# Attention of one batch and second experts of the batch before it, interleaved in 64 steps in which TensorE takes the attention's share first

## What is computed

```python
x = x + selective_state_space_block(layernorm(x))
x = x + experts(layernorm(x))      # first experts
x = x + attention_b(layernorm(x))  # a linear ("flow") attention of 16 heads over 1024 tokens
x = x + experts(layernorm(x))      # second experts

# experts: every one of 16 experts is computed for every token
probs = softmax(x @ router_w.T + router_b); top_p, top_i = top_k(probs, 6)
for e in range(16):
    out = out + x @ expert_w[e] * gate[:, e:e + 1]
```

## Time and profile before

| what | value |
|---|---|
| median of 3 runs | 4711.26 us (4708.32 to 4712.44) |
| the profiled execution's time | 4707.32 us |
| its span, first to last instruction | 4705.3 us |
| mean granted TensorE clock | 0.97 |
| PE busy | 4300.6 us, 91% |
| DVE busy | 3605.8 us, 77% |
| ACT busy | 3070.8 us, 65% |
| POOL busy | 2587.7 us, 55% |

### The profile page before, as it was taken

The page is one execution under the profiler, slowest core; times in us unless marked ns, Lnnn a source line. Parts: engine busy times, 40 slices in busy tenths (PEclk is TensorE's granted clock), DMA queues, the critical chain, the costliest instruction groups (busy, mean ns, idle before and its releaser), DMA issues.

```text
span 4705.3 us, 83840 instructions
## 1 busy us (share of the span) xinstructions
PE 4300.6 (91%) x22592; PEld 2989.4 (64%) x22592; DVE 3605.8 (77%) x9602; ACT 3070.8 (65%) x8898; POOL 2587.7 (55%) x1284
## 2 busy tenths in 40 slices
PE   4899999999999999999999999876777799999999
PEld 4777777777777777777777777433443444444444
DVE  3899999999999999999999998633423367777776
ACT  5888888888888888888888888244444411111111
POOL 3988888888888888888888888300000000000000
PEclk8999999999999999999999999888888899999999
DMA  2111111111111111111111111100110000000000
GB/s 95 57 58 54 55 52 59 52 58 56 52 55 52 59 58 53 55 52 59 52 58 56 52 55 53 41 27 27 47 33 27 28 27 19 19 18 18 18 18 17
DMA packets 119138, 211.87 MB, mean 45 GB/s; under 512 B 19232, under 2 KB 85664, under 8 KB 118560
## 3 DMA queue, kind: packets, MB, share of 16 engines
q1 hardware_dynamic: 119072, 211.10, 13.7%
HBM read 184.83 MB, written 26.21 MB: 45 GB/s over the span
## 4 chain that ended last, share of the span: by engine, by line
PE 52%; issue 17%; DVE 17%; ACT 9%; POOL 2%; DMA 1%; DVEq 1%; SPq 1%; POOLq 0%; ACTq 0%
PE ps L654 26%; ACT zr L403 5%; PE ps L705 5%; PE ps L631 5%; DVE macc L964 3%; PE ps L781 3%; PE ps L684 2%; PE ps L691 2%; PE ps L760 2%; POOL prod L342 1%; PE ps_dA L781 1%; DVE xcv L1072 1%; DVE zt L1084 1%; PE ps L661 1%; DVE dtt L1121 1%
## 5 line engine op out<-in xcount | busy, mean ns | idle before, releaser
L654 PE MATMUL ps<-w_x,mxT 128*128 128x512 f32 x4096 | 1875.0, 596 | 8.9 <-DVE macc L964 8.9
L874 DVE TENSOR_TENSOR_SCAN hb<-ps_dA,hb 128x1088 f32<-128x1088 f32 x512 | 1240.7, 2423 | 76.3 <-POOL hb L350 65.3
L342 POOL TENSOR_TENSOR prod<-hb,cbc 128x1024 f32<-128x1024 f32 x512 | 1122.9, 2193 | 253.6 <-DVE hb L893 252.5
L350 POOL TENSOR_TENSOR hb<-u,bbc 128x1024 f32<-128x1024 f32 x512 | 1201.1, 2346 | 75.1 <-POOL prod L342 70.9
L403 ACT ACTIVATE zr<-dt,aneg 128x128 f32<-128x128 f32 x4096 | 1240.8, 388 | 1.4 <-DVE dt L1010 1.1
L964 DVE SCALAR_TENSOR_TENSOR macc<-ps,gate,macc 128x256 f32<-128x256 f32 x2048 | 977.4, 477 | 276.3 <-PE ps L654 203.7
L654 PEld LDWEIGHTS ps<-w_x,mxT 128*128 128x128 f32 x4096 | 736.3, 191 | 699.1 <-issue 632.1
L631 PEld LDWEIGHTS ps<-prod,ident 128*128 128x128 f32 x8192 | 948.8, 193 | 121.0 <-POOL prod L342 74.2
L631 PE MATMUL ps<-prod,ident 128*128 128x128 f32 x8192 | 966.7, 276 | 12.6 <-POOL prod L342 12.5
L412 ACT ACTIVATE ps_dA<-zr 128x1024 f32<-128x1024 f32 x512 | 518.4, 1012 | 0.0
L455 ACT ACTIVATE macc<-x1b,ms 128x256 f32<-128x256 f32 x128 | 64.1, 501 | 438.7 <-DVE macc L964 423.4
(11 more groups left out here) (186 smaller groups left out, 4876.7 us busy)
## 6 DMA issues: line engine op xcount, KB each, us to landing
bbc<-bcd SPq DMA_DIRECT2D x128, 512.0 KB, 3.7
cbc<-bcd SPq DMA_DIRECT2D x128, 512.0 KB, 3.7
xt<-in_x SPq DMA_DIRECT2D x128, 128.0 KB, 3.6
x2d<-macc SPq DMA_DIRECT2D x64, 128.0 KB, 1.7
xcv<-x2d SPq DMA_DIRECT2D x64, 128.0 KB, 2.1
x3d<-x1b SPq DMA_DIRECT2D x64, 128.0 KB, 1.9
x1b<-x3d SPq DMA_DIRECT2D x64, 128.0 KB, 2.0
out_dram<-macc SPq DMA_DIRECT2D x64, 128.0 KB, 1.7
```

The lines of the kernel that those rows point to most:

```text
L342: TT(dst, states, cc, ALU.mult).then_inc(M["prodp"], 1)
L350: TT(hb[c % 2][:].rearrange("p (e n) s -> p e n s", e=EB)[:, :, :, 1:SL], u[k][:, :, t0:t0 + CH].rearrange("p e (n s) -> p e n s", n=1).br ...
L654: last = mm(banks[p % len(banks)][:], mxT[k][:, j, :], w_x[:, j, p * 512:(p + 1) * 512], start=(j == 0), stop=(j == KD - 1))
L874: V.tensor_tensor_scan(states, dA, states, 0.0, ALU.mult, ALU.add).then_inc(M["scan"], 1)
```

## The change

Stages 2 and 3 become one. It has 9 rounds b = 0 to 8 of 64 steps ("slots") each, written out and not looped. In round b, slot s = 8 t + p holds the s-th share of the attention of batch b and pair p of the experts of tile t of batch b-1. Round 0 has no experts, round 8 no attention. Within a slot PE does the attention's share first, then the expert pair; DVE does the expert sums first, then the routing's share, then the attention's; ACT does the routing's share, then the attention's. The expert banks in rounds 1 to 7 are two (G0, G1), the attention has one set of four (`QUAD`) and M1 for small results. The input tiles of a whole batch (`x_rows`) and the attention's result (`x3_rows`) stay in SBUF, in buffers of stage 1: `x3d`, its 64 stores and 64 loads, and the second loading of `x2d` for the residual are gone. `co` is done before `ci`; `so` waits for `l1` since it uses the same banks. ACT loads its tables where the two functions alternate.

```diff
+        def merged(slot):
+            for b in range(NB + 1):
+                for t in range(NT):
+                    for p in range(X // 2):
+                        slot(b, t, p)
+
+        def routed(b, t):
+            n = (b - 1) * NT + t + 1
+            return n if 0 <= n < NTILES else None
...
+            def slot(b, t, p):                       # PE
+                n = (b - 1) * NT + t
+                if b < NB:
+                    attend(b, t * (X // 2) + p)
+                if b > 0:
+                    experts_mm(n + NTILES, n % 2, p, p + 1, G4 if b == NB else G, fresh=(b == NB and t == 0))
+                m = routed(b, t)
+                if m is not None:
+                    if p == 2:
+                        route(m + NTILES, m % 2, M0)
+                    if p == 3:
+                        logits(m + NTILES, m % 2, M0)
...
+            def attend(b, s):                        # PE
...
+                if s == 11:
+                    pe.wait_ge(A["hm"], AHEAD + (b + 1) * 4)
+                    columns_of(0, "cv0")
...
+                if s == 23:
+                    pe.wait_ge(A["hn"], AHEAD + (b + 1) * 4)
+                    pe.wait_ge(A["cv"], AHEAD + b + 1)
+                    columns_of(4, "cw0")
+                if s in (24, 25):
+                    by_group((0, 1) if s == 24 else (2, 3), (mats[:, 6, :], mats[:, 7, :]), ka, "co",
+                             lambda m: pe.wait_ge(A["l2"], AHEAD + b * 4 + m + 1))
+                if s in (29, 30):
+                    by_group((0, 1) if s == 29 else (2, 3), (mats[:, 4, :], mats[:, 5, :]), qa, "ci",
+                             lambda m: pe.wait_ge(A["cs"], AHEAD + b * 4 + m + 1))
+                if 35 <= s < 35 + NT:
+                    t = s - 35
+                    pe.wait_ge(A["v"], AHEAD + (b + 1) * KD)
...
+                if s in (47, 48):
+                    pe.wait_ge(A["kvm"], AHEAD + (b + 1) * KD)
+                    by_group((0, 1) if s == 47 else (2, 3), (mats[:, 8, :], mats[:, 9, :]), r1, "om", lambda m: None)
+                if 51 <= s < 51 + NT:
+                    t = s - 51
+                    pe.wait_ge(A["og"], AHEAD + (b + 1) * 4)
                     pe.wait_ge(A["x2"], AHEAD + b * NT + t - 1)
                     for j in range(KD):
                         last = mm((BC, YP)[t % 2][:, 0:D], r2[:, j, t * P:(t + 1) * P], w_a[:, 3, j, :],
                                   start=(j == 0), stop=(j == KD - 1))
                     last.then_inc(A["om2"], 1)
+                    if b + 1 < NB:
+                        transposes((b + 1) * NT + t)   # waits for A["xn"] of that tile
...
+            def slot(b, t, p):                       # DVE
+                n, r = (b - 1) * NT + t, routed(b, t)
+                if b > 0:
+                    expert_sums(n + NTILES, n % 2, 2 * p, 2 * p + 2, G4 if b == NB else G)
+                if r is not None:
+                    if p == 0:
+                        v.wait_ge(A["x3"], AHEAD + r + 1)
+                        route_norm1(r + NTILES, x3_rows(r))
+                    if p == 4:
+                        route_scores(r + NTILES, r % 2, M0)
+                    if p >= 5:
+                        for q in range(4 * (p - 5), min(4 * (p - 4), 11)):
+                            route_step(r + NTILES, q)
+                    if p == 7:
+                        route_gate(r + NTILES, r % 2)
+                if b < NB:
+                    attend(b, t * (X // 2) + p)
...
+            def attend(b, s):                        # DVE
...
+                if s in (17, 18):
+                    weighted(b, (0, 1) if s == 17 else (2, 3), qa, r1, "r1", "qs", 20)
+                if s in (20, 21):
+                    weighted(b, (0, 1) if s == 20 else (2, 3), ka, r2, "r2", "ks", 24)
+                if s == 22:
...
+                    head_masks(b, 4, (34, 35, 32, 33), "hn")
...
+                if s in (25, 26):                    # two of four clips, waits for "co", makes "cs"
...
+                if s == 27:                          # TS(xTa, xTa, -1.0, None, ALU.max)
...
+                if s in (28, 29):                    # half of the maximum each
...
+                if s == 32:                          # reciprocal of the sums "e"
...
+                if s in (33, 34):                    # half of v each, makes "v"
...
+                if s == 46:
+                    v.wait_ge(A["kv0"], AHEAD + b + 1)
+                    for j in range(KD):
+                        TT(mats[:, 8 + j, :], M1[:, j * P:(j + 1) * P], hmask, ALU.mult).then_inc(A["kvm"], 1)
+                if s in (48, 49):                    # two of four TT(r2, QUAD[m], r2), makes "og"
...
+                if b + 1 < NB and 50 <= s < 50 + NT:
+                    norm((b + 1) * NT + s - 50)
+                if b + 1 < NB and 48 <= s < 48 + NT:
+                    sums((b + 1) * NT + s - 48)
+                    moments((b + 1) * NT + s - 48)
+                if 52 <= s < 52 + NT:
+                    t = s - 52
+                    n = b * NT + t
                     v.wait_ge(A["om2"], AHEAD + n + 1)
+                    TT(x3_rows(n), (BC, YP)[t % 2][:, 0:D], bo_row[:], ALU.add).then_inc(A["x2"], 1)
                     v.wait_ge(A["x2"], AHEAD + n + 1)
+                    TT(x3_rows(n), x3_rows(n), x_rows(n), ALU.add).then_inc(A["x3"], 1)
```

More of the change, by code:

```diff
@@ L297, in _, with batch @@
             sp.dma_start(hmask, dram["hmask"]).then_inc(s_wc, 16)
[L299 to L325, removed]
+            def batch(b):
+                for n in range(b * NT, (b + 1) * NT):
+                    sp.dma_start(x_rows(n), flat_tile(x2d, n)).then_inc(A["x"][b % 2], 16)
+            batch(0)
+            for b in range(NB + 1):
+                if b + 1 < NB:
+                    sp.wait_ge(A["x3"], AHEAD + b * NT)
+                    batch(b + 1)
+                for n in range(max(b - 1, 0) * NT, b * NT):
+                    sp.wait_ge(R["ac"], AHEAD + (n + NTILES + 1) * (X + 1))
+                    sp.dma_start(flat_tile(out, n), macc[n % 2][:]).then_inc(R["o"][n % 2], 16)
             for k in range(2):
-                sp.wait_ge(A["o"][k], AHEAD + NTILES // 2 * 16)
-            experts(x3d, out, NTILES)
+                sp.wait_ge(R["o"][k], AHEAD + NTILES * 16)
         @block.gpsimd
@@ L612, in _, with ln_exp, sigmoid @@
-            for t in range(NT + 1):
-                norm(0, t)
-            with a.Fori(0, NB - 1) as b:
-                attend(b, True)
-            attend(NB - 1, False)
-            experts(NTILES)
+            table = ["ln"]
+            def ln_exp():
+                if table[0] != "ln":
+                    nc.scalar.preload_act_table_set("natural_log_exp_and_others")
+                table[0] = "ln"
+            def sigmoid(o, x, **kw):
+                table[0] = "sigmoid"
+                return act(o, x, ACT.Sigmoid, **kw)
@@ L620, in _ @@
+            for n in range(NT):
+                norm_scale(n)
+                if n > 0:
+                    norm_copy(n - 1)
+            norm_copy(NT - 1)
+            merged(slot)
         @block.tensor
@@ L736, in _, with by_group, columns_of, transposes @@
             pipeline(pe, step)
[L738 to L750 removed]
             pe.wait_ge(s_wa, 16)
[L753 to L757 removed]
+            def by_group(ms_, lhs, src, done, before):
+                for m in ms_:
                     j, g = m // NG, m % NG
                     before(m)
[L760 to L764 removed]
+                    mm(QUAD[m][:], lhs[j], src[:, j, g * TG:(g + 1) * TG], start=True, stop=True).then_inc(A[done], 1)
+            def columns_of(first, done):
+                for m in range(4):
+                    last = mm(M1[:, m:m + 1], mats[:, first + m, :], c_eps6[:], start=True, stop=True)
+                last.then_inc(A[done], 1)
+            def transposes(n):
+                t = n % NT
                 pe.wait_ge(A["xn"], AHEAD + n + 1)
@@ L829, in attend @@
                     last.then_inc(A["om2"], 1)
-                    if more and t > 1:
-                        transposes(b + 1, t - 2)
-                if more:
-                    transposes(b + 1, NT - 2)
-                    transposes(b + 1, NT - 1)
-            for t in range(NT):
-                transposes(0, t)
-            with pe.Fori(0, NB - 1) as b:
-                attend(b, True)
-            attend(NB - 1, False)
-            experts(NTILES)
+                    if b + 1 < NB:
+                        transposes((b + 1) * NT + t)
[9 more added lines that the diff above has]
+                        route(m + NTILES, m % 2, M0)
+                    if p == 3:
+                        logits(m + NTILES, m % 2, M0)
+            for n in range(NT):
+                transposes(n)
+            merged(slot)
         @block.vector
@@ L1265, in _ @@
+            for n in range(NT):
+                sums(n)
+                moments(n)
+                if n > 0:
+                    norm(n - 1)
+            norm(NT - 1)
```

(5 more changed lines are left out.)

473 lines of the change are left out of this document (199 added, 274 removed).

## The result

The changed kernel takes 4804.07 us (median of 4 runs, 4803.46 to 4805.44), the one before 4711.05 us on the same chip (4 runs, 4708.32 to 4712.44): ratio 1.0199, 95% interval 1.0181 to 1.0216. It is 2.0% slower. Predicted were 4840 us (4720 to 4940), 2.7% slower. The profiled execution took 4805.44 us, its span is 4803.4 us, the mean granted clock 0.966.

The account below looks back on a forecast made before the run. PE, standing for DVE's slot before, was taken to bound merged rounds. Start 3052, round 0 87, six rounds 1362, seventh 216, last experts 115.4, switch 1, end 2.2: span 4835.6, so 4840 us (4720 to 4940).

Parts of the forecast that it names:

- the gain of 34 us per round: Merged rounds: most the change can bring if PE never waits, 172 us against 206.0 before.
- The work, 172 us: PE's work in a merged round at full clock: attention 56.8 us plus experts 115.4.
- Idle, 38 us: PE's waits per merged round for DVE's slot before, at `hn`, `v`, `kvm`, `og`, `xn` and six `x2`: sum 37.8.
- Clock, 17 us: Merged round: clock falls after PE's waits in slots 23, 35, 47, 51 and 53 to 58 cost 17 us, ends 0 and 30.
- Six rounds of 227: Six merged rounds, each work 172, idle 38 and clock 17 us, together 1362 us.
- Round 0, 87 us: Attention alone: 87 us instead of 90.6, as `co` before `ci` saves 3.4 and no residual loads are awaited.
- Seventh round and switch, 217: Last round with attention, without a next norm, 216 us, and 1 us for the switch to the last experts.
- Last experts and end, 117.6: After the merged rounds: experts of the last batch 115.4 us and the end 2.2.
- Table loads, banks, `x3d`: Two more ACT table loads a round are covered, two expert banks add nothing, `x3d` transfers were already hidden.
- Clock hardly falls: Rival: merged rounds idle as forecast, but the clock costs only 0 to 5 us each; 4725 to 4760 us, chance 0.20.
- Faster: Rival: DVE's slots don't hold PE, idle and clock together below 36 us a round; chance 0.10.
- Worse: Rival: clock at half through most of slots 23 to 30 and 47 to 58, 30 us a round or more; 4930 up, chance 0.12.

Follow-up runs that it names:

- experiment 1: Changed kernel, but in each slot PE does the expert pair first and the attention's share after it: 4551.48 us, ratio 0.9668 to the kernel before.
- experiment 7: Changed kernel with PE's pair first and `om2`, transposes and the next batch's statistics and norm one slot later: 4527.73 us, ratio 0.9621 to the kernel before.
- experiment 4: Changed kernel with 17 unused matmuls a round on PE ahead of the waits for `x2`: 4752.18 us, ratio 1.0094 to the kernel before.
- experiment 2: Changed kernel, but DVE does the attention's share before the sums and the routing: 4622.15 us, ratio 0.9818 to the kernel before.
- experiment 5: Changed kernel, but DVE does the routing last (sums, attention, routing): 4788.11 us, ratio 1.0174 to the kernel before.
- experiment 8: The kernel of experiment 7 with the routing last on DVE: 4531.59 us, ratio 0.9623 to the kernel before.
- experiment 9: The kernel of experiment 8 with the routing last on ACT too: 4546.07 us, ratio 0.9661 to the kernel before.
- experiment 10: The kernel of experiment 7 with the routing last on ACT alone: 4563.21 us, ratio 0.9694 to the kernel before.
- experiment 3: Changed kernel with `om2`, transposes and the next batch's statistics and norm one slot later, `x2` unmoved: 4657.56 us, ratio 0.9894 to the kernel before.

## Why the prediction was right

**Direction and mechanism: shown.** It said that waits one slot back eat the gain of 34 us per round, at `hn`, `v`, `kvm`, `og` and six times at `x2`, and that all are DVE's. The rows of after have these and little else, and the first experiment, which lengthens that distance by one pair, takes three quarters of the waiting away. Of the signs that the prediction named, one failed: the clock of the merged stage is 0.93, not below 0.9. That the time is off by only 36 us is in part luck: the seven merged rounds were put 46 us too long and the other terms 14 us too short.

**Point by point**, from the span 4835.6 forecast to 4803.4 measured, 32.2 less:

- *The work, 172 us.* Right: 174.5 with the clock at 0.99 (experiment 7), so a part of the 2.5 us can still be the clock's.
- *Idle, 38 us.* Measured 32.5 in round 4075.26 to 4293.70 (218.44 less 185.97). Forecast against measured: `hn` 5.9, 5.05; `v` 4.2, 2.96; `kvm` 2.8, 2.33; `og` with `xn` of slot 50 4.4, 2.31 + 0.18; `xn` of slot 51 0.9, 0.84; the six `x2` 3.5, 3.3, 3.7, 3.8, 3.1, 2.2 against 3.16, 2.90, 3.32, 3.46, 2.83, 1.91. Each `x2` is 0.3 to 0.4 short of its forecast: the sum was made of durations, but DVE's instructions start up to 0.1 us before the one ahead ends (the norm of 0.41 was followed after 0.33). Over the longer chain ahead of `v` it comes to more: from the end of slot 25's pair (4123.6) to `v` DVE took 23.2 us where the forecast had 24.7, and PE 20.3 where it had 20.4. Not forecast were 0.94 us for ACT's `mxT` and 0.27 for `mxn`: I had gone through the waits of `attend` alone, not those of the routing's `route` and `logits`. At `hn` it is another thing. From the end of slot 18's pair (4097.36) DVE took 13.8 us, more than the forecast's 12.8 to 13.2, with 1.52 of it idle until slot 20's pair was done; but PE took 8.7 and not 7.4, since a wait of 0.94 for `mxT` and the routing's products lie in these slots:

```profile
4100.24 0.62 PE L653 MATMUL ps_dA<-w_r,mxT 128*128 128x16 f32 x4 [0.94 <-ACT mxT L421]
...
4102.71 1.07 DVE L977 SCALAR_TENSOR_TENSOR macc<-ps,gate,macc 128x256 f32<-128x256 f32 x2 [1.52 <-PE ps L665]
...
4111.15 1.87 PE L761 MATMUL ps_dA<-c_eps,prod 128*128 128x1 f32 x8 [5.05 <-DVE prod L1179]
```

- *Clock, 17 us.* Round 220.0 less 174.5 of work less 32.7 idle (mean of six) leaves 12.8. (Half of five chances of 2.8 is 7.0 and not the 7.5 of the sum, which changes little.) A typical round has 11.5; one of the six took 225.4 with PE busy 192.7 in it. The loss lies between the ends 0 and 30, and the clock falls at most of the places where I expected it, as the 4110 and 4205 stretches show; behind `kvm` it stayed at 1.00 (4175 to 4185).
- *Six rounds of 227.* 1322.2 instead of 1362 (3149.57 to 4471.79). This is the term that made the prediction too high, by 40 us: 5.3 us of idle and 4.2 of clock too many a round, 2.5 of work too few.
- *The start.* The first projection is at 3054.06 (3052).
- *Round 0, 87 us.* 95.5. The 3.4 us for `co` before `ci` came: PE's wait for `v` fell from 10.0 to 6.6. But I had left out the one-slot distance of `x2` here, where no pair lies between: six waits of 1.4 took the place of seven for `mxn` of 0.7, 3.5 us more, and PE's busy time is 70.7 instead of 65.9 at a clock of 0.82 instead of 0.86.
- *Seventh round and switch, 217.* 210.6.
- *Last experts and end, 117.6.* 121.05 (4682.35 to 4803.4). PE waits there for `mxn` 6 times 0.25 us; the rest of the 3.4 us I can't put down to rows.
- *Table loads, banks, `x3d`.* No wait of PE is put down to them. In the two banks no pair of the six rounds waits for its sums; the one such wait, 1.2 us, is at the switch to four banks, for which the forecast had 1.

**The rivals.** *Clock hardly falls* is refuted by the clock rows and by experiment 4. *Faster* would have needed less than 36 us of idle and clock together; it was 45.5. *Worse* would have needed 30 us of clock a round. By estimate the waits alone would have made about a draw (174.5 + 32.7 = 207.2 us a round against 206.0 before); with the clock's 12.8 it is a loss.

The Trainium skill (TensorE: Matmul & The Clock Gate, section "Loop structure matters more than you think") says that a long wait between matmuls lets PE go cold, and its example is a wait for DMA. The runs agree for these waits for DVE and give it a size: from the changed kernel to experiment 1, with PE's idle time down by 25.5 us a round, the same work costs PE 11.5 us a round less and the clock rises from 0.93 to 0.99.

## What to carry to other kernels

When two streams are interleaved slot by slot on engines that work strictly in order, ask for each wait how many slots lie between its release and its use, and put the share that nobody waits for (here the pair) in front of the one that depends on another engine: that order was worth 253 us here, 5%, while the load of the engines was the same. Here merging a stage with idle time and a full one paid only once such distances were longer: this kernel went from 4711 to 4804 us as first written, to 4658 with one more slot of distance for `x2`, to 4622 with DVE's attention share first, to 4551 with PE's pair first and to 4528 us (3.8% faster than before) with the pair first and the slot of distance. A reordering on one engine passes the wait on to the next one (ACT in experiments 2, 5 and 8 to 10), so look at the whole list of waits and not at the one row that you wanted to shrink.

## What the hardware showed unexpectedly

Useless matmuls in a wait made the kernel faster: 102 us of added PE work took 52 us off the time (4804.07 to 4752.18), because the remaining work ran some 50 us faster. And the clock's part in a wait is large. The six rounds of experiments 1, 2 and 3, in this order, columns as above (those of the changed kernel stand with experiment 4):

```profile
3192.56:4290.14 1097.58, 1054.58 (x3122) 518.26 (x3121) 691.42 (x2304) 354.75 (x876) 0.00 (x0) 0.99 0.04 11
```
```profile
3190.14:4354.88 1164.74, 1080.21 (x3122) 527.09 (x3120) 693.28 (x2304) 351.84 (x876) 0.00 (x0) 0.96 0.03 11
```
```profile
3176.43:4383.70 1207.27, 1079.79 (x3122) 527.72 (x3121) 693.59 (x2304) 352.24 (x876) 0.00 (x0) 0.97 0.03 10
```

PE's idle time fell by 25.5, 18.6 and 11.4 us a round and its busy time for the same work by 11.5, 7.3 and 7.3, so that each us of waiting taken away brought 0.4 to 0.6 us more.
